# Attention's preparation and the expert work moved between the attention steps of a post-norm layer

## The reference

```python
x = layernorm(x + attention(x))        # 16 heads of 8, q and k RMS-normed and rotated, causal softmax, @ w_proj.T
x = layernorm(x + peer(x))

# peer, per token
xn = rmsnorm(x) * norm_w
q = xn @ w_q.T                          # 8 heads, two halves each
sim1, sim2 = q halves . keys            # 32 keys a half
s1, i1 = top_k(sim1, 8); s2, i2 = top_k(sim2, 8)
fs, pk = top_k(all 64 sums s1 + s2, 8)  # fi: the 8 expert numbers of a head, out of 1024
hidden = gelu(xn . expert_down[fi]) * relu(fs)
out = sum over heads and k of hidden * expert_up[fi]
```

## Time and profile before

| | |
|---|---|
| runs | 1782.3 us median of 3 (1781.9 to 1787.96) |
| profiled execution | 1787.43 us, its span 1785.5 us |
| VectorE (DVE) busy | 1507.0 us, 84% |
| TensorE (PE) busy | 1353.2 us, 76%, mean granted clock 0.818 |
| ScalarE (ACT) busy | 938.5 us, 53% |
| GpSimd (POOL) busy | 750.4 us, 42% |

### The profile page before, as it was taken

How to read it: one execution, slowest core, us unless ns; L and a number is a source line. 1 busy time by engine, 2 the same in 40 slices (tenths; PEclk the granted TensorE clock), 3 DMA queues, 4 the chain that set the end, 5 groups by cost and what they waited for, 6 DMA issues and landing times. The chain is left out here.

```text
span 1785.5 us, 53337 instructions
## 1 busy us (share of the span) xinstructions
PE 1353.2 (76%) x19632; PEld 929.3 (52%) x19632; DVE 1507.0 (84%) x6821; ACT 938.5 (53%) x1646; POOL 750.4 (42%) x1088
## 2 busy tenths in 40 slices
PE   3557588787968778796877869697887869688556
PEld 2323265554646555464645646474655546465436
DVE  2136898989899898989989899998989998988994
ACT  0647463755556475564647465564737555563110
POOL 1216353444635353453525355463534446352320
PEclk7688879797888879788887969888796978878665
DMA  3000000000000000000000000000000000000000
GB/s 77 1 6 8 6 8 8 14 8 1 15 7 15 7 14 8 1 15 7 15 7 14 8 2 15 6 15 7 15 8 14 8 1 15 1 15 1 8 7 9
DMA packets 29976, 18.59 MB, mean 10 GB/s; under 512 B 1824, under 2 KB 29216, under 8 KB 29728
## 3 DMA queue, kind: packets, MB, share of 16 engines
q1 hardware_dynamic: 29728, 15.23, 3.0%
HBM read 11.04 MB, written 4.19 MB: 9 GB/s over the span
## 5 line engine op out<-in xcount | busy, mean ns | idle before, releaser
L585 ACT ACTIVATE prob<-S 128x512 f32<-128x512 f32 x640 | 367.0, 598 | 298.8 <-PE OV L790 160.4
L869 PE MATMUL G<-whot,onehot 128*128 128x16 bf16 x12288 | 378.4, 172 | 48.3 <-DVE hid L1266 27.6
L869 PEld LDWEIGHTS G<-whot,onehot 128*128 128x128 bf16 x12288 | 365.7, 100 | 81.5 <-issue 23.5
L1228 DVE TENSOR_TENSOR onehot<-lo_no,esel 128x1024 bf16<-128x1024 uint16 x512 | 373.9, 785 | 0.2 <-issue 0.2
L422 POOL TENSOR_TENSOR qk_a<-qk_n,cosw 128x256 f32<-128x256 f32 x64 | 59.4, 928 | 482.6 <-DVE qk_n L1047 446.6
L839 PE MATMUL F<-xn,downT 128*128 128x512 f32 x256 | 153.9, 758 | 96.1 <-ACT hid L530 96.1
L777 PE MATMUL S<-causal,ident_b 128*128 128x128 bf16 x1024 | 209.1, 236 | 2.3 <-issue 2.3
L468 POOL TENSOR_TENSOR gat<-gat,cande 128x1280 f16<-128x1280 f16 x64 | 151.4, 2366 | 110.4 <-DVE gat L1189 110.4
L775 PE MATMUL S<-qT,kT_even 128*128 128x512 bf16 (+3 forms) x512 | 154.1, 332 | 50.9 <-ACT prob L585 42.3
L727 PE MATMUL S<-ident_b,stack 128*128 128x128 bf16 x1024 | 94.6, 261 | 106.1 <-POOL stack L438 72.9
L1169 DVE FIND_INDEX8 topi<-topv,sims 128x8 uint16<-128x32 f32 x1024 | 166.2, 185 | 0.0
(11 more groups left out here) (136 smaller groups left out, 2608.6 us busy)
## 6 DMA issues: line engine op xcount, KB each, us to landing
xa<-in_L_attn_x SPq DMA_DIRECT2D x16, 256.0 KB, 2.8
xr<-in_L_attn_x SPq DMA_DIRECT2D x16, 256.0 KB, 2.9
out<-r SPq DMA_DIRECT2D x16, 256.0 KB, 2.9
onehot<-in_L_ffn_expert_down SPq DMA_DIRECT2D x1, 512.0 KB, 5.9
up<-in_L_ffn_expert_up SPq DMA_DIRECT2D x1, 512.0 KB, 7.0
onehot<-in_L_ffn_keys SPq DMA_DIRECT2D x1, 256.0 KB, 6.3
onehot<-in_L_attn_w_qkv SPq DMA_DIRECT2D x1, 192.0 KB, 4.7
onehot<-in_L_attn_w_proj SPq DMA_DIRECT2D x1, 64.0 KB, 4.6
```

The source lines that it names most:

```text
L585: act.activation(dst, src, ACT.Exp, scale=SCALE).then_inc(exp_done.sem, 1)
L869: last = nc.tensor.matmul(bank[:, 16 * i:16 * i + 16], onehot[:, pair, t, :], whot[:, t, w_part, :], start=(w_part == 0), stop=(w_part == 2))
L1228: dve.tensor_tensor(onehot[:, pair, t:t + 8, :].rearrange("p t (c i) -> p t c i", i=2), lo, e, ALU.is_equal)
```

## The change

The stretch behind the 40 steps is dissolved. Its TensorE work stands between the steps of the next turn, by step numbers. Attention of b keeps the last head group's product for step 1 of turn b + 1. In turn b + 1 follow the output projection, norm and all similarities and choices of b, with the first 8 one-hots; in turn b + 2 the hidden products, the other one-hots, all parts and VectorE's products with chunks 0 to 6; in turn b + 3 its product with chunk 7, the expert output and the second norm. q and k of b + 1 are projected at step 3 of turn b, rotated before they are normalised (the root is multiplied in after), both halves at once, and transposed by head group at steps 25, 29, 33 and 39. One inverse root serves q and k, the first norm and the second.

The values have a projection of their own at step 1. The sum of the selected numbers is no longer taken on GpSimd and VectorE: `turn_numbers` adds the 20 candidates on TensorE, 20 products a tile. The score banks get one mask product where they hold two diagonal blocks. The expert output goes to the second G bank. ScalarE has no idle activations for its tables any more.

```diff
-        SIMS_UNIT = 4
-        SELECTION_STEP = 34
-        WEIGHT_STEPS = list(range(1, 9)) + list(range(13, 29))
+        QK_STEPS = [25, 29, 33, 39]
+        SIMS_STEPS = [9, 11, 17, 21]
+        NUMBER_STEPS = [22, 27, 32, 35]
+        SELECTION_STEP = 36
+        WEIGHT_STEPS = [n for n in range(5, 39) if n not in (21, 31)]
...
 gather (GpSimd)
-                pool.tensor_tensor(g, g, cande[:, t % 2].unsqueeze(3).to_broadcast([P, H, NCAND, TOPK]), ALU.mult)\
-                    .then_inc(gat_done.sem, 1)
-                pool.wait_ge(gat_done.sem, gat_done.value(b, 2 * t + 1))
-                pool.tensor_tensor(g[:, :, 0:10], g[:, :, 0:10], g[:, :, 10:20], ALU.add)\
+                pool.tensor_tensor(g, g, cande[:, t % 2].rearrange("p h c -> p c h").unsqueeze(3)
+                                   .to_broadcast([P, NCAND, H, TOPK]), ALU.mult)\
                     .then_inc(gat_done.sem, 1)
...
 scores (TensorE)
                     for half, kc, col in blocks:
                         pe_k = kT[half][:, j, kc * P:(kc + 1) * P]
                         nc.tensor.matmul(bank[:, col:col + T - kc * P], pe_k, qT[:, j, kc * P:T],
-                                         start=True, stop=False, skip_group_check=True)
-                        last = nc.tensor.matmul(bank[:, col:col + P], ident_b[:, :], causal[:, :],
-                                                start=False, stop=True, skip_group_check=True)
-                    last.then_inc(s_ready.sem, 1)
+                                         start=(col == 0), stop=False, skip_group_check=True)
+                    if len(blocks) == 2:
+                        diagonal = bank[:, :].rearrange("p (c n) -> p c n", n=P)[:, 0:NT:blocks[1][2] // P]
+                        mask = causal[:, :].unsqueeze(1).to_broadcast([P, 2, P])
+                    else:
+                        diagonal, mask = bank[:, 0:P], causal[:, :]
+                    nc.tensor.matmul(diagonal, ident_b[:, :], mask, start=False, stop=True, skip_group_check=True)\
+                        .then_inc(s_ready.sem, 1)
...
+            def turn_numbers(b, t):
+                rows = slice(t % 2 * 64, t % 2 * 64 + 64)
+                pe.wait_ge(gat_done.sem, gat_done.value(b, t + 1))
...
+                for c in range(NCAND):
+                    last = nc.tensor.matmul(F_SEL[rows, t // 2 * P:(t // 2 + 1) * P], gat[:, t % 2, c].rearrange("p h k -> p (h k)"),
+                                            ident_b[:, :], start=(c == 0), stop=(c == NCAND - 1),
+                                            skip_group_check=True)
+                last.then_inc(numbers_turned.sem, 1)
...
 weights (TensorE)
                 if quarter == 0:
                     pe.wait_ge(g_free.sem, g_free.value(b, chunk - 1))
+                    if chunk == 1:
+                        pe.wait_ge(ln2.sem, ln2.value(b, 1 - ln2.per_batch))
...
 iteration (TensorE), in the loop over the 40 steps
+                    if step == 1:
+                        if late is not None:
+                            attend(late, NG - 1)
+                        if b is not None:
+                            project_v(b, nxt)
+                        if nxt is not None:
+                            transpose_x(nxt, b)
+                    if step == 2:
+                        if oldest is not None:
+                            expert_outputs(oldest, range(2))
+                        if late is not None:
+                            transpose_o(late, NG - 1)
+                    if step == 3:
+                        if nxt is not None:
+                            project_qk(nxt, 0, b)
+                            project_qk(nxt, 1, b)
+                        if oldest is not None:
+                            expert_outputs(oldest, range(2, NT))
+                        if late is not None:
+                            turn_outputs(late)
+                    if step == 4:
+                        if late is not None:
+                            project_out(late)
+                        if older is not None:
+                            hidden_products(older)
                     if older is not None and step in WEIGHT_STEPS:
-                        weights(older, 8 + WEIGHT_STEPS.index(step))
+                        weights(older, WEIGHT_STEPS.index(step))
+                    if step == 8 and late is not None:
+                        transpose_yi(late)
...
 iteration (GpSimd)
+                    keep_rows(older)
+                    rotate(nxt, 0)
+                    rotate(nxt, 1)
+                    rests(nxt, 0)
+                    rests(nxt, 1)
                     candidates(late, 0)
+                    third_parts(nxt, 0)
+                    third_parts(nxt, 1)
                     candidates(late, 1)
                     gather(late, 0)
...
 iteration (ScalarE), n is the step
+                    if n == 4 and older is not None:
+                        for c in range(NHI):
+                            hidden(older, c)
+                    if n == 9 and late is not None:
+                        normed(late)
+                    if n == 10:
+                        if late is not None:
+                            similarities(late, 0)
+                            norm1_rows(late)
...
+                    if nxt is not None and n in (13, 14):
+                        first_parts(nxt, n - 13)
+                    if nxt is not None and n in (16, 17):
+                        second_parts(nxt, n - 16)
...
+                    if nxt is not None and n in QK_STEPS:
+                        transposed(nxt, QK_STEPS.index(n))
```

More of the change, by code:

```diff
@@ L736, in shift_by_maxima @@
+            def shift_by_maxima(b, last):
+                pe.wait_ge(kT_done.sem, kT_done.value(b, NG))
+                if last is not None:
+                    pe.wait_ge(o_done.sem, o_done.value(last, NG - 1))
                 for t in range(NT):
@@ L931, in iteration @@
[L931 to L940 removed]
+                    if nxt is not None and step in QK_STEPS:
+                        transpose_stack(nxt, QK_STEPS.index(step), b)
```

745 lines of the change are left out of this document (352 added, 393 removed).

## The result

The changed kernel takes 1938.1 us (median; 1936.8 to 1939.6), against 1783.1 for the kernel before on the same chip: a ratio of 1.086 (95% interval 1.084 to 1.089). The forecast was 1767 with a range up to 1845. What the change was to take from VectorE it took; the time came back as waits.

The account below looks back on a forecast made before the run. VectorE was taken as the bound; 76.3 us of work plus 14.3, 2.4, 3.1, 6.0 and 1.2 made a 103.3 us turn. Span 324 + 14 T gave 1770, forecast 1767 us; 8-in-10 range 1665 to 1845.

Parts of the forecast that it names:

- Term b: From norm1 to the first keys: chain of 4.9 us beside 2.5 of VectorE work, so 2.4 us of waiting a turn.
- TensorE has room for both at its high clock: TensorE can take the number products (4.8 us a batch) and the merged masks (nothing).
- Term a: Tail chain (chain a), TensorE from step 30's wait for chunk 4 to the selection: 14.3 us, VectorE idling 9.6.
- Term e: TensorE's clock: half speed after pauses could lengthen its chains; 1.2 us a turn taken, bounds 0 and 13.3.
- Rival 2: TensorE's low clock falls on the chains: turn 108.7 us, whole 1843; chance 0.17.
- Term d: GpSimd beside VectorE: rotations cost the root 4.5 us, gathers beside one-hots 1.5; 6.0 a turn, bounds 0 and 7.2.
- Rival 3: Rotations hold the root whole: 7 us instead of 4.5, turn 105.8, whole 1802; chance 0.14 together with rival 4 (half a change).
- Term c: Smaller VectorE waits, 3.1 us a turn: last head group's output 0.7, norm2 1.2, first pairs 1.2.
- VectorE's own savings: Sums, one inverse root and an add go: 8.1 us a turn off VectorE, busy near 1380 us instead of 1507.0.
- merging masks: On TensorE, takes 24 instructions and no column away; forecast to gain nothing.
- The ends: First scores at 65 us, turn 0 60, turn 1 65, turns 2 and 15 5 under a like turn, last stretch 148.
- What the forecast would have looked wrong by: Decode waiting under 4 us, like turns under 98 or over 108 us, or turn 0 not near 60.

Follow-up runs that it names:

- e1: Changed kernel with ScalarE reading the late batch's first similarities ahead of step 10's exponentials; 1928.5 us, ratio 1.082 to the kernel before.
- n1: Kernel before, in its old order, with only the sums of the selected numbers moved to TensorE; 1850.8 us, ratio 1.037.
- g2: n1 with only one of the twenty number products of each tile left on TensorE; 1763.3 us, ratio 0.989 to the kernel before.
- f2: f1 with ScalarE's row operations of the norms moved from step 10 to step 18; 1837.0 us, ratio 1.030 to the kernel before.
- g1: f2 with the selected numbers summed on VectorE again and TensorE's 80 small products gone; 1844.3 us, ratio 1.034 to the kernel before.
- e2: Changed kernel with VectorE's weighting of chunk 4 put ahead of the late batch's last top keys and pairs; 1890.7 us, ratio 1.060.
- e4: Changed kernel with GpSimd's rotation done on one eighth of the elements; 1887.1 us, ratio 1.059 to the kernel before.
- m2: Changed kernel with a separate mask product for each block of a score bank again; 1936.9 us, ratio 1.085 to the kernel before.
- f1: e2 with TensorE's transposes of the normed tokens moved from step 8 to 11, behind the attention product; 1914.1 us, ratio 1.072.
- h2: f2 with TensorE's number products at steps 28, 34, 36 instead of 27, 32, 35, selection at 37; 1749.8 us, ratio 0.980.
- k3: h2 with the first two number products moved later, to steps 24 and 29; 1767.9 us, ratio 0.991 to the kernel before.

## Why the prediction was wrong, point by point

- **The sum itself.** The span was 165 us above the 1770 forecast: 14 x (112.7 - 103.3) = 132 from the like turns, and 33 from the ends. VectorE's work in a like turn was forecast right: 76.3, 4.65 beside chain a and 6.0 for contention are 87.0, and 86.8 were measured. All of the 9.4 us a turn are waits, and terms b and a have most of them.
- **Term b failed.** The step is "step 10's scores 0.3, exponential 0.6, copy 0.6": the exponential has no wait in it, but it is the first of its group and waits for the attention product of step 11 (6.42 us in the row above). The forecast walked TensorE's and VectorE's queues and took ScalarE's durations without its queue. 2.4 forecast, 9.1 measured.
- **And its size is not its price.** By the forecast's own way of adding, e1 should have given back 5 us a turn; it gave 0. What e1 shows is that a wait of VectorE does not count where the next things that it needs hang on the same link. This is the deeper error of the sum "VectorE's work plus its waits".
- **"TensorE has room for both at its high clock" failed.** In the old order 4.8 us a turn of products turned a saving into a loss of 66 us (n1), and without nearly all of them the kernel is 88 us faster (g2). That is the old order: with the other moves made and mended (f2) the numbers on TensorE cost nothing clear (g1), and in the changed kernel itself they were not taken back. How much of its 155 us is theirs stays open; as the moves interact, no split is shown.
- **Term a** had the right mechanism (step 30's wait for chunk 4; e2 removes it and gains 3.6 us a turn) and was too small: from step 30's part (1089.91) to the landing (1106.94) it took 17.0 instead of 14.3 us, and VectorE waited 12.2 instead of 9.6 (2.1 at a product with a chunk, 6.4 at an o, 3.7 at the decode). The attention product in it is 1.7 of the 2.7 more: it ran at a granted clock of 0.58, 4.0 us instead of 2.3 (from the chain of waits):

```profile
1091.35 4.00 PE OV L836 x32
```

- **Term e**, 1.2 us for the clock, was the right kind of cost put too low, as the row just named shows: before, 60 of the 64 attention products took 2.34 us and none over 2.65, and the mean of a matmul was 434 ns; after, it is 523, 2.6 us a turn more. Rival 2 named the clock; taken alone it would have explained 5 us a turn of the 9.4. Its sign, half the clock over the last quarter of each turn, did not come: the quarters of the like turn from 1000.7 had 0.97, 0.64, 0.93 and 0.85, the low one from TensorE's stand for norm1 on (1035 to 1042: 0.50). What no rival named is a queue on ScalarE and GpSimd in the chain.
- **Term d was right.** Contention on the root was put at 4.5 us for the rotations; seven eighths of them gave 4.0 (e4). Rival 3, that they hold the root whole (the Trainium skill, "SBUF — State Buffer", section "Who interferes with whom"), would have given 7 x 7/8 = 6.1. The 4.0 speaks against its full size, not against its mechanism. Its sign, root steps of 0.6 us and more, came in three of the eleven (0.75, 0.82, 0.82 between 1027.8 and 1031.8); the last six ran behind the rotations, at about 0.30. Only 6.1 us of the rotations ran beside the root at all, and GpSimd's own operations grew there too (1.17 to 1.27 us, before the root 0.73). The same step of the root after and in e4:

```profile
1029.60 0.82 DVE L1081 TENSOR_TENSOR qk_t<-qk_ms,qk_rs 128x140 f32<-128x140 f32 x1
```

```profile
669.00 0.29 DVE L1081 TENSOR_TENSOR qk_t<-qk_ms,qk_rs 128x140 f32<-128x140 f32 x1
```

- **Term c**: 1.9 for the last group's o (0.7 forecast), 1.5 for norm2 (1.2), 0.3 for the first pairs (1.2): together 3.7 against 3.1.
- **VectorE's own savings** were right (1385.3 busy, near 1380 forecast), and merging masks is nothing, as forecast (m2).
- **The ends.** First scores at 64.8 us (65). Turn 0 took 65.7 from there (60), turn 1 82.5 (65), where VectorE stands 16.4 us for batch 0's last o, 9.6 for the first keys and 5.7 and 5.2 in the tail; turn 2 3.5 more than "a like turn less 5", turn 15 8 less; the tail 159.1 from the last attention product against 144 (148 from the landing, 4 earlier). At the end of turn 1 the kernel was 32 us ahead of the one before (213.0 against 244.7) and not 55.
- **What the forecast would have looked wrong by** came about: like turns above 108 us, turn 0 at 65.7 and not near 60, the longest of VectorE's waits the first keys and not the decode, and a decode that waits 3.7 us, under 4. The last was to mean that chain a is not there. It was there (12.2 us), with most of its wait ahead of the decode, so that sign was badly chosen.

## What to carry to other kernels

Before adding up one engine's work and waits, write down for each queue what stands ahead of each instruction that somebody waits for, ScalarE and GpSimd included; an in-order engine that waits early delays everything behind, and the wait that the profile shows is often one of several on the same link. Take such a wait away by moving the waiting instruction behind work that others need (the numbers at steps 28, 34 and 36 instead of 27, 32 and 35: 87 us), and expect nothing from a move until the chain crosses it: the same edit gave 0, 25 and 87 us in three orders. An engine with 20% idle time can still be on the chain; only leaving its work out shows what its microseconds cost. And look at VectorE's own work after each move as well: where it lands beside GpSimd's, a wait that was saved can be lost again (f1).

## What the runs showed of the hardware

- The attention product (32 matmuls with nine output rows) is 2.34 us at a granted clock of 1.00 and 4.03 at 0.58, and which of a turn's four products are long changes with the order. One of its matmuls in f2, h2 and k3, whole run (busy us, mean ns):

```profile
L837 PE MATMUL OV<-prob,vp 128*9 128x512 f32 (+3 forms) x2048 | 206.3, 558 | 0.7 <-ACT prob L623 0.7
```

```profile
L837 PE MATMUL OV<-prob,vp 128*9 128x512 f32 (+3 forms) x2048 | 179.6, 497 | 0.9 <-ACT prob L623 0.7 <-issue 0.2
```

```profile
L837 PE MATMUL OV<-prob,vp 128*9 128x512 f32 (+3 forms) x2048 | 192.6, 528 | 0.7 <-ACT prob L623 0.7
```

- Less waiting of TensorE can come with more than its length: f2 to h2, 2.2 us a turn of gather waits gone (2.6 to 0.4), 6.8 us of turn gained, and the granted clock of the like turns 0.94 instead of 0.89.
- GpSimd's small adds of 64 and 32 elements a partition take 0.30 and 0.25 us, and 0.72 and 0.70 beside VectorE's one-hots (944.87 to 947.5 in e1). With two conversions before them, four such adds took 4.0 us (943.63 to 947.64) instead of 1.7 (938.53 to 940.21):

```profile
940.00 0.25 POOL L485 TENSOR_TENSOR candv<-topv 128x32 f32<-128x32 f32 x1
...
944.98 0.72 POOL L479 TENSOR_TENSOR candv<-topv 128x64 f32<-128x64 f32 x1
...
946.99 0.70 POOL L485 TENSOR_TENSOR candv<-topv 128x32 f32<-128x32 f32 x1
```
